# Gated-delta attention and ternary feed-forward on one core: seven half-block products in the third token group as well, with the work around it re-placed

## What is computed

```python
# x: (2, 1024, 512); K = 64, V = 128; w1, w2: (1408, 512); w3: (512, 1408)
x = x + gated_delta(layernorm(x))
x = x + ffn(layernorm(x))

def gated_delta(x):
    q, k, v = x @ Wq, x @ Wk, x @ Wv
    beta, delta = sigmoid(x @ Wb + bb), softplus(x @ Wd + bd)
    for t in range(T):                       # scan over 1024 tokens
        S = beta[t][:, None] * S + delta[t][:, None] * outer(k[t], v[t])
        out[t] = q[t] @ S
    return out @ Wo

def quantize(w):                             # every entry becomes -1, 0 or 1
    return clip(round(w / (mean(abs(w)) + 1e-8)), -1, 1)

def ffn(x):
    h = sigmoid(x @ quantize(w1).T) * (x @ quantize(w2).T)
    return h @ quantize(w3).T
```

## Time and profile before

| | us |
|---|---|
| runs, median of 3 | 326.93 |
| the profiled execution | 326.43 |
| its span, first to last instruction | 324.7 |
| PE busy | 315.7 (97% of the span) |
| DVE, ACT, POOL busy | 219.5, 157.0, 134.5 |
| group 1: block units, down part | 46.6, 19.0 |
| group 2: block units, down part with the wait behind it | 46.2, 20.4 |
| group 3: block units | about 34 |

### The profile page before, as it was taken

The page is one execution under the profiler, slowest core; times in us unless marked ns, Lnnn a source line. Parts: engine busy times, 40 slices in busy tenths (PEclk is TensorE's granted clock), DMA queues, the critical chain, the costliest instruction groups (busy, mean ns, idle before and its releaser), DMA issues.

```text
span 324.7 us, 6312 instructions
## 1 busy us (share of the span) xinstructions
PE 315.7 (97%) x2284; PEld 189.0 (58%) x2284; DVE 219.5 (68%) x489; ACT 157.0 (48%) x325; POOL 134.5 (41%) x375
## 2 busy tenths in 40 slices
PE   7999999999999999999999999999999979999996
PEld 6888779865435444445454444454544437888545
DVE  6889899899998757366589643688897502554401
ACT  3687897789855671333143260222252115777300
POOL 7298325599913016990021045700281531435300
PEclk9999999999999999999999999999999999999999
DMA  6999900657841523300003041000006160000011
GB/s 198 371 389 397 362 3 0 89 108 131 123 91 32 115 49 68 108 19 2 0 2 65 2 112 52 35 0 2 2 0 113 65 145 36 2 0 3 1 67 65
DMA packets 48880, 27.81 MB, mean 86 GB/s; under 512 B 40656, under 2 KB 41424, under 8 KB 48848
## 3 DMA queue, kind: packets, MB, share of 16 engines
q1 hardware_dynamic: 48528, 27.40, 31.5%
q10 hardware_dynamic: 320, 0.00, 0.1%
HBM read 13.89 MB, written 4.19 MB: 56 GB/s over the span
## 4 chain that ended last, share of the span: by engine, by line
PE 77%; DVE 11%; ACT 4%; issue 3%; POOL 3%; DMA 1%; DVEq 0%; POOLq 0%; ACTq 0%
PE ffn L1568 29%; PE ffn L1597 15%; PE ffn L1615 8%; PE ffn L1413 6%; PE lev L1489 3%; PE pd L1615 3%; DVE w_nat L1102 2%; PE pd L1423 2%; DVE X L1115 2%; PE lev L1500 2%; PE lev L1446 2%; PE pd L1597 1%; DMA w_nat<-x_all 1%; PE ffn L1401 1%; PE oc L1473 1%
## 5 line engine op out<-in xcount | busy, mean ns | idle before, releaser
L1568 PE MATMUL ffn<-w_nat,w12T 128*128 128x512 f16 x528 | 117.2, 379 | 0.5 <-DVE xnT L1315 0.4
L1568 PEld LDWEIGHTS ffn<-w_nat,w12T 128*128 128x128 f16 x528 | 50.6, 98 | 62.1 <-issue 3.2
L1597 PE MATMUL ffn<-w3T,w_nat 128*128 128x512 f16 x308 | 67.3, 379 | 0.0
L1597 PEld LDWEIGHTS ffn<-w3T,w_nat 128*128 128x128 f16 x308 | 30.1, 98 | 37.1 <-ACT w_nat L909 1.0
L522 POOL TENSOR_TENSOR ve<-mv,rconst 128x2 f32<-128x2 f32 x12 | 2.5, 212 | 109.8 <-DVE mv L1019 109.8
L903 ACT ACTIVATE xnT<-ffn 128x512 f32<-128x512 f32 x33 | 19.6, 593 | 57.5 <-PE ffn L1568 57.3
L1304 DVE SCALAR_TENSOR_TENSOR x_sb<-ffn,x_sb 128x512 f32<-128x512 f32 (+1 forms) x15 | 10.1, 673 | 40.6 <-PE ffn L1597 38.6
L1315 DVE SCALAR_TENSOR_TENSOR xnT<-ffn,xnT 128x512 f32<-128x512 f32 x33 | 22.6, 685 | 21.8 <-PE ffn L1568 21.4
L1413 PE MATMUL ffn<-xnT,w_proj 128*128 128x256 f32 x128 | 29.5, 384 | 1.2 <-ACT xnT L718 0.8
L1413 PEld LDWEIGHTS ffn<-xnT,w_proj 128*128 128x128 f32 x128 | 23.7, 190 | 5.1 <-issue 1.0
L1320 DVE TENSOR_TENSOR w_nat<-xnT,w_nat 128x512 f16<-128x512 f32 x33 | 25.0, 757 | 0.3
(11 more groups left out here) (184 smaller groups left out, 508.0 us busy)
## 6 DMA issues: line engine op xcount, KB each, us to landing
x_sb<-in_L_attn_x_dram SPq DMA_DIRECT2D x16, 256.0 KB, 8.0
out_dram<-x_sb SPq DMA_DIRECT2D x15, 256.0 KB, 2.0
w_nat<-in_L_ffn_w_dram SPq DMA_DIRECT2D x2, 1536.0 KB, 12.0
w_nat<-in_L_ffn_w_dram SPq DMA_DIRECT2D x2, 1408.0 KB, 15.6
w_nat<-in_L_ffn_w_dram SPq DMA_DIRECT2D x2, 1280.0 KB, 12.8
w_proj<-in_L_attn_Wv_dram SPq DMA_DIRECT2D x1, 256.0 KB, 5.2
wo<-in_L_attn_Wo_dram SPq DMA_DIRECT2D x1, 256.0 KB, 13.9
out_dram<-x_sb SPq DMA_DIRECT2D x2, 128.0 KB, 1.7
```

The source lines that it names most:

```text
L1568: done = nc.tensor.matmul(bank[n % 3][:, :], w12T[:, a * DT + t, u * P:(u + 1) * P], xT(g)[:, part, t, :], start=t == 0 and part == 0, sto ...
L1597: done = nc.tensor.matmul(down_bank(g, m)[:, :], hid_at(g, part, j, m), w3T[:, j, :], start=n == 0, stop=n == 2 * HT - 1)
```

## The change

- `FAST = (2, 3)`: group 2 is made with seven half-block products as well. Group 1 becomes the group in front of a fast one, and group 2 a fast group that also carries the attention of chunks 6 and 7.
- Chunk 6's levels and chain (the first attention work of a fast group) sit in the down part of the group before: levels in unit 13 of group 1, chain0 in its unit 11, chain1 in its unit 13; before, they sat in units 2 and 0 of group 2.
- POOL fetches chunk 6's factors in group 1 ahead of chunk 5's norm2. For the odd chunk of a group (5 and 7) the sums of tokens and their low part are made by DVE (`sums`, `xloS`), no longer by POOL.
- In group 2 the statistics of chunk 7 are split over three places (`norm2a`, `norm2b`), with a new slot of DVE behind the last block.
- The fourth weight sum moves from unit 11 to unit 13, now of group 1. ACT loads the sigmoid table again right behind chunk 7's exponentials.

```diff
--- before.py
+++ after.py
@@ -33,7 +33,7 @@
     QU = 4
     SL = WN // QU
     XS, XS_FAST = 2048.0, 512.0
-    FAST = (3,)
+    FAST = (2, 3)
     HP = 2 * P
     HS = 64.0
     ROUND = 1.5 * 2.0 ** 23
@@ -266,20 +266,21 @@
         SP_AFTER = {"turn": (7, 12)}
 
         DOWN = 2 * HT
-        DVE_NEXT_FAST = DVE_AFTER | {"xlo": (8, 13)}
+        DVE_NEXT_FAST = {k: v for k, v in DVE_AFTER.items() if k != "xlo"}
+        DVE_NEXT_FAST |= {"sums": (None, 12), "xlo": (8, 12), "xloS": (None, 12)}
         ACT_NEXT_FAST = {"gt": (2, 7), "oT": (4, 9), "xhiN": (7, 12), "xhiS": (8, 13)}
         SP_NEXT_FAST = {"turn": (9, 13)}
 
-        PE_FAST = {"levels": (-1, 5), "o": (1, 8), "wo": (2, 9)}
-        DVE_FAST = {"chain0": (-2, None), "chain1": (-1, None),
+        PE_FAST = {"levels": (-2, 5), "o": (1, 8), "wo": (2, 9)}
+        DVE_FAST = {"chain0": (-4, None), "chain1": (-2, None),
                     "chainA": (None, 2.5), "chainB": (None, 3), "chainC": (None, 3.5), "chainD": (None, 4),
                     "chainE": (None, 4.5), "masks0": (0, 6.5), "masks1": (0, 7), "masks2": (0, 7.5),
-                    "masks3": (0, 8), "state": (2, None), "resid0": (5, 10.5), "resid1": (6, 11),
-                    "xlo": (DOWN, DOWN + 2), "xloS": (None, DOWN + 2), "norm2a": (8.5, DOWN), "norm2b": (9, DOWN),
-                    "apply": (10, DOWN + 1), "sums": (None, DOWN + 1)}
+                    "masks3": (0, 8), "state": (2, None), "resid0": (5, 10.5), "resid1": (5.5, 11),
+                    "xlo": (DOWN, DOWN + 1), "xloS": (None, DOWN + 1), "norm2a": (8.5, 11.5), "norm2b": (9, HT + 1),
+                    "apply": (10, DOWN), "sums": (None, DOWN)}
         ACT_FAST = {"gt": (0, None), "oT": (2, 9), "xhiN": (HT, HT + 2), "xhiS": (HT + 1, HT + 2)}
-        POOL_FAST = {"fetch": (-1, 0), "sums0": (10, None), "sums1": (11, None), "xlo": (HT + 1, None),
-                     "norm2": (9, HT + 1)}
+        POOL_FAST = {"fetch": (-1, 0), "sums0": (10, None), "sums1": (11, None), "norm2": (9, HT + 1),
+                     "xlo": (HT + 1, None)}
         SP_FAST = {"turn": (HT + 1, HT + 2)}
 
         def placed(plain, next_fast, fast):
@@ -306,7 +307,7 @@
         R12_POOL, R3_POOL = (9, 10), (4, 5, 6, 7)
         R3_AT = {2: (0, 1), 3: (2, 3)}
         EXPS_AT = {(0, 11): (4, 5), (0, 13): (6,), (1, 12): (7,)}
-        T_AT = {2: (3,), 3: (2,), 4: (4,), HT: (1,)}
+        T_AT = {2: (3,), 3: (2,), 4: (4,), HT + 2: (1,)}
         GATES_AT = {(0, 11): (4,), (0, 12): (5,), (0, 14): (6,), (1, 13): (7,)}
         R3_CUT = (0, 5 * P, H)
 
@@ -677,14 +678,16 @@
                     gates(5)
                     gates(6)
                 fetch(2 * g + 3)
-                for c in (2 * g + 2, 2 * g + 3):
-                    norm2(c)
-                    if is_fast(c):
-                        sums0(c)
-                        sums1(c)
-                    xlo(c)
+                norm2(2 * g + 2)
+                if g + 1 in FAST:
+                    sums0(2 * g + 2)
+                    sums1(2 * g + 2)
+                xlo(2 * g + 2)
                 if g + 2 < G and g + 1 in FAST:
                     fetch(2 * g + 4)
+                norm2(2 * g + 3)
+                if g + 1 not in FAST:
+                    xlo(2 * g + 3)
                 if g == 1:
                     gates(7)
 
@@ -919,6 +922,8 @@
                         nc.scalar.preload_act_table_set("natural_log_exp_and_others")
                     for c in EXPS_AT.get((g, u), ()):
                         exps(c)
+                    if (g, u) == (1, 12):
+                        nc.scalar.preload_act_table_set("sigmoid_and_others")
 
             def seed(g, u):
 
@@ -1377,6 +1382,8 @@
                         hidden_lo(g, k - 2)
                     if k > 0:
                         up_a(g, k - 1)
+                for s, c in DVE_AT.get((g, HT + 1), ()):
+                    attn(s, c)
                 hidden_lo(g, HT - 1)
                 for u in range(HT, UNITS):
                     for s, c in DVE_AT.get((g, DOWN + u - HT), ()):
```

## The result

Four runs of the changed kernel gave 332.26 to 333.72 us, median 332.99; four of the kernel before a median of 326.94. The ratio is 1.0175, 95% interval 1.0141 to 1.021: slower by 6 us, outside the range given. The profiled execution took 333.21 us, 1.7 of them outside its span.

What follows compares the result with a forecast made beforehand. TensorE, busy 97% of the span, was taken as the bound, if other engines deliver in time. Terms -4.7 + 2.2 + 0.5 + 0.3 + 2.5 = +0.8 us gave 327.7 us, range 324.2 to 331.0.

Steps and rivals of the forecast that it cites:

- all three waits: TensorE waits about 2 us before chunk 6's levels, half a microsecond at product 3, 4 to 5 us before group 3.
- Products, -4.7: Group 2's blocks: seven half-block products instead of plain ones save 0.43 us in each of eleven blocks, -4.7 us.
- End of group 1, +2.2: Group 1's down part: TensorE waits for chunk 6's chain, late on VectorE behind ScalarE's copy S; +2.2 us, bounds 1 and 3.5.
- The transposes come out even: End of group 1: chunk 5's transposes land at 204.2, just when TensorE wants them; no cost, upper bound 1 us.
- Start of group 2, +0.5: Block 0 of group 2: masks on VectorE delay up_b, so product 3 waits; +0.5 us, bounds 0 and 1.
- Units of group 2, +0.3: Units 3 and 4: chain levels on VectorE slow GpSimd's multiply and so product 7; +0.3 us, bounds 0 and 3.
- the rival of GpSimd's pace: Group 2: VectorE's work stretches GpSimd's multiply to 1.32 us in every unit; +2.7 us, 330.4 us; chance 0.2.
- End of group 2, +2.5: Before group 3: TensorE waits 4.6 us instead of 2.08 for chunk 7's transposes, queued on SP and DMA engines; +2.5 us.
- The clock, a rival with 0.1: Behind the long wait before group 3, TensorE's clock falls and products slow; +2.7 us, 330.4 us; chance 0.1.

Runs made afterwards that it cites:

- e7: Changed kernel with chunks 6 and 7's transposes one place earlier on SP, chunk 7's exponentials and tables one unit later, chunk 6's low part S on VectorE: 321.75 us.
- e11: Changed kernel with FAST = (3,), so group 2 is made with 16 products of 512 columns and the other re-placements around group 3 stay: 324.6 us.
- e4: Changed kernel with 56 matmuls of unused result filling TensorE's wait before group 3, after a wait for the last residual sum: 331.16 us.
- e8: Changed kernel with only chunk 6's transposes one place earlier on SP, ahead of group 2's first store: 328.73 us.
- e12: Changed kernel with chunk 7's apply and sums behind group 2's first add_out on VectorE again, its low parts behind the second: 325.63 us.
- e10: The kernel of e7 with three of chunk 6's masks ahead of group 1's last add_out on VectorE: 321.04 us.
- e1: Changed kernel with the transposes of chunks 6 and 7 one place earlier on SP, each ahead of a store: 325.98 us.

## Why the prediction was wrong

The sum was +0.8 us, the profiled executions' spans differ by +6.8. The places of all three waits were right. The 6.0 us between are: products 1.0 less gain, end of group 1 1.2 more, start and units of group 2 0.4 less, end of group 2 2.2 more, and 2.0 for the clock, a rival given 0.1 and not in the sum. So two steps failed outright: the queue at the end of group 2, where the stores' DMA time was put at nothing, and the clock behind the long wait, left out of the sum. The products' gain and chunk 5's transposes were mis-sized beside them.

- **Products, -4.7.** Measured -3.7 with all that moves along (from the change's trace, and from e7 against e11). Added up from start to start over group 2, the 308 half-block products of e7 take 34.3 us, 0.1115 each and not the 0.110 of group 3's window, and the 176 whole ones of before 38.4, 0.218 and not 0.219: -4.1. The other 0.4 is in the starts around them: the 172 down products of groups 1 and 2 take 0.26 us more in e7 than in e11, being broken up more often there, and the wait of 0.19 costs 0.32 from start to start (198.70 plus 18 times 0.218 is 202.62; the product starts at 202.94).
- **End of group 1, +2.2.** The wait for the chain is 1.87, with the release as forecast: the copy S ended at 195.64 (195.6 forecast), VectorE's low part, `add_out` and three levels behind it. "The transposes come out even" failed, and just past its bound of 1 us: they were issued at 197.90 and 199.43 as forecast, but landed some 5.9 us after the second issue rather than 4.8. e4, e8 and e12 show what that costs at full clock, 1.25, 1.21 and 1.26 us. In all 3.4 instead of 2.2.
- **Start of group 2, +0.5.** 0.42, right, and e10 shows the cause. One count in it was off: product 3 stands behind eight further products, not nine, and a break of 0.2 us; the 5.0 us are right (205.47 to 210.48), the nine would give 5.3.
- **Units of group 2, +0.3, and the rival of GpSimd's pace.** No wait: ten units in 37.86 us. The eleven multiplies of each of GpSimd's two kinds took 0.74 and 0.78 us on average in group 2, 0.74 and 0.73 in group 3. The longest were three of 0.91, two beside chain levels and one beside an apply, all short of the 1.0 from which the rival decides. I had given this way 0.2. The prediction also read the earlier trace rows wrongly: the operation of 1.32 us stood beside VectorE's low part N, not beside a chain level, and chunk 6's low part S (3.72 us) beside low parts as well. VectorE in the kernel before, at the time of that operation:

```profile
258.10 1.02 DVE L1218 TENSOR_TENSOR w_proj<-x_all,w_proj 128x768 f16<-128x768 f32 x1
```

GpSimd in the changed kernel, a multiply beside two chain levels and a sum beside `hidden_lo`, and that `hidden_lo` on VectorE:

```profile
216.75 0.91 POOL L644 TENSOR_TENSOR xnT<-xnT,q 128x256 f32<-128x256 f32 x1
...
248.38 1.21 POOL L627 TENSOR_TENSOR x_all<-x_all 128x256 f32<-128x256 f32 x1
```

```profile
248.30 0.69 DVE L1370 TENSOR_TENSOR w_nat<-xnT,w_nat 128x512 f16<-128x512 f32 x1 [0.18 <-ACT w_nat L979]
```

So the contention that the Trainium skill's GPSIMD Engine Reference (Key points) states does show in this stage. It cost nothing because `hidden_lo`, which stretches most, met a multiply for no more than 0.2 us in group 2 (at 223.90 and 231.15, multiplies of 0.80 and 0.81). The rival had VectorE beside the multiply in every unit; that is the step of it that failed.
- **End of group 2, +2.5.** The step that failed most: +4.66. Up to SP the count held: statistics at +7.2 us from the start of unit 10 (7.3 forecast), scale +10.5 (9.7; two of its six small operations took 0.42 and 0.79 us beside VectorE), low part +13.0 (12.4), `add_out` from +15.8 to +16.5 (15.9), chunk 6's transposes +16.9 (16.3). From there to chunk 7's landing I took 6.1 + 4.9 = 11.0 us and it was 12.6. I had counted the two pairs' own DMA time but put the stores' at nothing: one (259.88) goes ahead of the first pair, one (264.60) between the pairs. The DMA view of 255 to 275 us of the changed kernel has

```profile
q1 hardware_dynamic: 7728, 2.62, 65.5%
out_dram<-x_sb SPq DMA_DIRECT2D x3, 256.0 KB, 3.3
```

that is 13.1 us of all engines: twice the 4.9 of the earlier trace rows and three stores of some 1.1 us. Two of these stand in front of the end of chunk 7's pair. 0.6 (late on SP) and 1.6, less 0.1 by which TensorE came later than forecast, make the 2.1 us between a wait of 4.6 and one of 6.74. That the 1.6 are the stores' is worked out from this view; no run moved a store alone. The cause behind these sizes is the order on VectorE and on SP together: e12 and e1, each by itself, take out 7 us with the clock's share.
- **The clock, a rival with 0.1.** It was the mechanism as written, +2.03 against my 2.7. That the size came near is luck in part: the windows view gives the stretch of the earlier trace rows a granted clock of 1.00, so nothing shows that it was one of fallen clock. And it belongs to the long wait as a consequence, not beside it as a mishap of its own chance. Having forecast 4.6 us of waiting, over twice the longest seen, I should have put it into the sum: with the 2.0 that were measured it is 329.7, still short by 3.3. TensorE: Matmul & The Clock Gate (part 1) of the Trainium skill, the rule named in the prediction, holds here: fall to half (0.43 us for a 512-column product) behind idling, none in e4 where the idle time was filled.
